# Sheaf and messages: 20 of each chunk's 125 columns are summed by source node in PSUM with one-hot matmuls, 105 are scatter-added

## The reference, cut to what matters

```python
# layer 1, "sheaf": a message for each end of each edge
msg_s = coef[:, None] * einsum('eij,ej->ei', L_sd, xd)
msg_d = coef[:, None] * einsum('eji,ej->ei', L_sd, xs)
out = x - zeros.at[src].add(msg_s) - zeros.at[dst].add(msg_d)
# layer 2, "messages": the index that is summed over is again src (row = edge_index[0])
m = silu(einsum('ei,ej,ijh->eh', x[dst], edge_attr, W_msg_tp) * norm)
agg = segment_sum(m, src)        # W_msg_lin is applied to the sums
```

## Time and profile before

| | |
|---|---|
| median of 3 runs | 31851.1 |
| lowest, highest | 31823.72, 31895.67 |
| the profiled execution's own time | 31882.81 |
| its span | 31881.0 |
| POOL busy | 24070.9 (76%) |
| DVE, PE, ACT busy | 9032.8 (28%), 8456.2 (27%), 1931.1 (6%) |
| PE's mean granted clock, 1.0 is 2.4 GHz | 0.651 |

### The profile page before, as it was taken

How to read it: one execution, slowest core, us unless ns; L and a number is a source line. 1 busy time by engine, 2 the same in 40 slices (tenths; PEclk the granted TensorE clock), 3 DMA queues, 4 the chain that set the end, 5 groups by cost and what they waited for, 6 DMA issues and landing times. The chain is left out here.

```text
span 31881.0 us, 172734 instructions
## 1 busy us (share of the span) xinstructions
PE 8456.2 (27%) x50463; PEld 7422.1 (23%) x50463; DVE 9032.8 (28%) x14173; ACT 1931.1 (6%) x4785; POOL 24070.9 (76%) x20072
## 2 busy tenths in 40 slices
PE   0000001000000644444444444244443443400003
PEld 0000001000000533333433333144443443200003
DVE  1434342111111433333333333121221211233332
ACT  0000000000000100000000000011111110000000
POOL 5777775777776788888888888778888886477776
PEclk9999998555555555555555555576676775655556
DMA  2111110111111111111111111222222221466664
GB/s 71 31 27 31 27 31 18 25 27 27 25 28 18 11 11 11 11 11 11 11 11 11 11 11 10 14 28 13 11 13 11 11 11 13 144 204 204 204 206 136
DMA packets 2304292, 1387.61 MB, mean 44 GB/s; under 512 B 1186461, under 2 KB 2150386, under 8 KB 2286402
## 3 DMA queue, kind: packets, MB, share of 16 engines
q0 software_dynamic: 1385008, 606.86, 16.8%
q10 hardware_dynamic: 814800, 576.02, 5.7%
q1 hardware_dynamic: 103746, 195.36, 1.8%
HBM read 666.59 MB, written 710.23 MB: 43 GB/s over the span
## 5 line engine op out<-in xcount | busy, mean ns | idle before, releaser
L1044 POOL DMA_INDIRECT acc<-column_sums,sum_rows x6250 | 10345.1, 1655 | 1936.1 <-issue 1879.4
L656 POOL DMA_INDIRECT gathered<-gat_table,src_index x6250 | 6525.8, 1044 | 2052.3 <-issue 2052.3
L1806 POOL DMA_INDIRECT gathered<-message_table,src_index x3125 | 3055.3, 978 | 984.7 <-issue 951.7
L1229 POOL DMA_INDIRECT gathered<-sheaf_table,src_index x3125 | 3011.5, 964 | 1026.4 <-issue 1025.3
L985 PE MATMUL column_sum<-edge_values,equal_src 128*128 128x16 f32 x6250 | 1363.6, 358 | 4857.3 <-ACT column_sums L1023 3410.7
L985 PEld LDWEIGHTS column_sum<-edge_values,equal_src 128*128 128x128 f32 x6250 | 1424.7, 332 | 4871.5 <-issue 3418.8
L511 PE MATMUL transposed<-ident,last_rows 128*128 128x128 f32 (+3 forms) x5 | 2.2, 442 | 8780.6 <-DVE sums L543 8780.6
L511 PEld LDWEIGHTS transposed<-ident,last_rows 128*128 128x128 f32 (+3 forms) x5 | 0.7, 149 | 8781.8 <-DVE sums L543 8781.8
L703 DVE TENSOR_TENSOR scores<-alpha_dst,gathered 128x375 f32<-128x375 f32 (+1 forms) x50 | 35.5, 710 | 6215.2 <-DMA gathered<-gat_table,src_index 6215.2
L998 DVE TENSOR_TENSOR equal_src<-src_row,src_chunk 128x512 f32<-128x512 f32 (+1 forms) x800 | 543.1, 679 | 4321.5 <-PE src_row L969 4304.3
L969 PE MATMUL src_row<-ident,src_chunk 128*128 128x128 f32 x6250 | 1559.5, 429 | 0.0
(11 more groups left out here) (335 smaller groups left out, 16084.8 us busy)
## 6 DMA issues: line engine op xcount, KB each, us to landing
message_rows<-gathered ACTq DMA_DIRECT2D x250, 1600.0 KB, 10.6
gathered<-gat_table,src_index POOLq DMA_INDIRECT x6250
acc<-column_sums,sum_rows POOLq DMA_INDIRECT x6250, 3.0
gat_rows<-scanned ACTq DMA_DIRECT2D x25, 3375.0 KB, 10.7
gat_rows<-scanned ACTq DMA_DIRECT2D x25, 2125.0 KB, 7.0
start_values<-starts SPq DMA_DIRECT2D x50, 1062.5 KB, 5.0
gathered<-sheaf_table,src_index POOLq DMA_INDIRECT x3125, 2.4
gathered<-message_table,src_index POOLq DMA_INDIRECT x3125, 2.9
```

The source lines that it names most:

```text
L656: g.indirect_dma_start(G[b][:, j, :], None, tab, bass.IndirectOffsetOnAxis(ap=IX[b][:, j:j + 1], axis=0)).then_inc(s_g[b], 16)
L1044: g.indirect_dma_start(self.acc[s * PER_SET + i], bass.IndirectOffsetOnAxis(ap=o.IXS[b][:, j:j + 1], axis=0), o.SV[b][:, j, :], None, comp ...
L1229: g.indirect_dma_start(G[b][:, j, :], None, self.tab17, bass.IndirectOffsetOnAxis(ap=IX[b][:, j:j + 1], axis=0)).then_inc(s_g[b], 16)
L1806: g.indirect_dma_start(G[b][:, j, :], None, self.qtab, bass.IndirectOffsetOnAxis(ap=IX[b][:, j:j + 1], axis=0)).then_inc(s_g[b], 16)
```

## The change

In both stages only the first 105 columns of a chunk (`SC`) go the old way. The last 20 (`MT`) are added in PSUM over the whole stage, in `o.acc`, four banks, 128 x 1568: partition is the low 7 bits of the source, the column is one of 16 features and one of 98 high parts. For each such column ("tile" below):

- DVE makes two one-hot matrices (`onehot`): low bits, 128x128 fp32, and high part, 128x98 bf16. Six small instructions per chunk split the sources into bits (`src_bits`).
- ACT writes the high one-hot times the edge's value for each of the 16 features (`place`: 16 activations of 98 columns, whose scale is a value per partition).
- PE multiplies (`tile_sum`: four fp32 matmuls of 392 columns, eight instructions).

The tiles of chunk k are worked in chunk k+1, the last chunk's after the stage. In the sheaf all 20 come in a row, between the hidden products and the equality groups, on both PE and ACT. In the messages one is put at the end of each of the first 20 steps on each engine. To make room in PSUM, the messages' four pairs of tiles (transposes, products, rows, sums) are single, and in the sheaf the rows share the two tiles of the hidden products, the sums share the tile of the transposes, and the second products have one tile. At the end of a stage DVE copies `o.acc` to SBUF, SP stores it as an eleventh accumulator, and `sum_accumulators` reads it too. The setup makes a row of 0 to 127.

```diff
+MT = 20
+SC = CH - MT
     def scatter_buffers(self, c, find_first):
-        o.groups = -(-CH // 4)
+        o.groups = -(-SC // 4)
+        o.NO = MT if find_first else 2
+        o.OL = sb("low_onehot", [P, o.NO, P])
+        o.OH = sb("high_onehot", [P, o.NO, NT], BF16)
+        o.MV = [sb(f"placed_values{b}", [P, D, NT]) for b in range(2)]
+        o.acc = self.ps("node_sums", [P, 4, 512], c)
+    def src_bits(self, v, w, o, src, b):
+        w(v.tensor_copy(o.LOI[:], src))
+        w(v.tensor_scalar(o.LOI[:], o.LOI[:], P - 1, None, ALU.bitwise_and))
+        w(v.tensor_copy(o.LO[b][:], o.LOI[:]))
...
+    def onehot(self, v, o, b, i):
+        r = i % o.NO
+        v.tensor_scalar(o.OL[:, r, :], self.iota_f[:], o.LO[b][:, i:i + 1], None, ALU.is_equal)
+        return v.tensor_scalar(o.OH[:, r, :], self.iota_f[:, 0:NT], o.HI[b][:, i:i + 1], None, ALU.is_equal)
+    def place(self, a, o, k, i, value):
+        n = k * MT + i
+        if not (first(k, 1) and i < 2):
+            a.wait_ge(o.s_tile, n - 1)
+        for d in range(D):
+            last = self.nc.scalar.activation(o.MV[i % 2][:, d, :], o.OH[:, i % o.NO, :], ACT.Copy, scale=value(d))
+        last.then_inc(o.s_mv, 1)
+    def tile_sum(self, pe, o, k, i):
+        n = k * MT + i
+        pe.wait_ge(o.s_mv, n + 1)
+        for m in range(4):
+            last = pe.matmul(o.acc[:, m, 0:4 * NT], o.OL[:, i % o.NO, :], o.MV[i % 2][:, 4 * m:4 * m + 4, :].rearrange("p d h -> p (d h)"),
+                             start=first(k, 1) and i == 0, stop=False, skip_group_check=True)
+        last.then_inc(o.s_tile, 1)
...
     def scatter_pool(self, g, o, k, b):
-        rounds = CH // PER_SET
+        rounds = SC // PER_SET
...
     def sheaf_edges   # PE, behind the eight groups of hidden products; ACT has tiles(k - 1) there too
+                        if not first(k, 1):
+                            tiles(k - 1)
                         self.scatter_pe(pe, o, k)
     # DVE, behind the copies of the gathered rows
+                        if not first(k, 1):
+                            onehots(k - 1, 1 - b, w)
+                        self.src_bits(v, w, o, srcc[:, SC:CH], b)
...
     def message_edges   # PE
-                        for s in range(GR + LAG):
+                        for s in range(GR + 1):
                             if s < GR:
                                 transposes(k, s)
+                            if s < GS:
                                 src_rows(k, s)
-                            if 1 <= s <= GR:
+                            if 1 <= s:
                                 second(k, s - 1)
-                            if s >= LAG:
+                            if LAG <= s < GS + LAG:
                                 sums(k, s - LAG)
+                            if s < MT and not first(k, 1):
+                                self.tile_sum(pe, o, k - 1, s)
     # ACT, last in its step s (before it: copy of transposes s, silu s-1, copy of sums s-3)
+                            if s < MT and not first(k, 1):
+                                placed(k - 1, s)
     # DVE, last in its step q (before it: outer product q, equality q)
+                            if q < MT and not first(k, 1):
+                                tile_onehot(k - 1, 1 - b, q)
```

More of the change, by code:

```diff
@@ L945, in scatter_buffers @@
         o.find_first = find_first
-        o.groups = -(-CH // 4)
-        o.VAL = sb("edge_values", [P, CH, D])
-        o.SV = [sb(f"column_sums{b}", [P, CH, D]) for b in range(2)]
-        o.IXS = [sb(f"sum_rows{b}", [P, CH], I32) for b in range(2)]
+        o.groups = -(-SC // 4)
+        if not find_first:
+            o.VAL = sb("edge_values", [P, CH, D])
+        o.SV = [sb(f"column_sums{b}", [P, SC, D]) for b in range(2)]
+        o.IXS = [sb(f"sum_rows{b}", [P, SC], I32) for b in range(2)]
         o.nq = 2 if find_first else 4
@@ new lines, in tile_sum, with keep_sums @@
+    def tile_sum(self, pe, o, k, i):
[5 more added lines that the diff above has]
+        last.then_inc(o.s_tile, 1)
+    def keep_sums(self, v, o):
+        v.wait_ge(o.s_tile, NCH * MT)
+        kept = o.MV[0][:].rearrange("p d h -> p (d h)").rearrange("p (h d) -> p h d", d=D)
+        for m in range(4):
+            v.tensor_copy(kept[:, :, 4 * m:4 * m + 4], o.acc[:, m, 0:4 * NT].rearrange("p (d h) -> p h d", d=4)).then_inc(o.s_out, 1)
@@ L1074, in _ @@
                     v.memset(zer[:], 0.0).then_inc(s_z, 1)
-                    for i in range(len(self.acc)):
+                    for i in range(len(parts)):
                         v.wait_ge(s_in[i % 2], 16 * (i // 2 + 1))
@@ L1248, in products @@
                             pe.wait_ge(s_xt, k * SG + (q + 1))
-                            if not first(k, 1) or q >= 2:
-                                pe.wait_ge(s_vc, k * SG + (q - 1))
+                            if not first(k, 1) or q >= 1:
+                                pe.wait_ge(s_vc, k * SG + q)
                             def second(j):
@@ L1265, in products, with tiles @@
                             second(3)
+                        if not first(k, 1):
+                            tiles(k - 1)
                         self.scatter_pe(pe, o, k)
+                    def tiles(k):
+                        pe.wait_ge(o.s_oh, k + 1)
+                        for i in range(MT):
+                            self.tile_sum(pe, o, k, i)
                     chunks(pe, NCH, 3, products)
+                    tiles(NCH - 1)
                 @block.scalar
@@ L1283, in step @@
                                 nc.scalar.activation(R[j % 2][:], pre[j % 2][:], ACT.Relu, bias=b1[:]).then_inc(s_r, 1)
+                        if not first(k, 1):
+                            tiles(k - 1, 1 - b)
                         self.scatter_act(a, o, k, b)
@@ L1286, in step, with tiles @@
                         a.dma_start(outv[:, ds(at, CH), :], OUT[b][:]).then_inc(s_o[b], 16)
+                    def tiles(k, b):
+                        a.wait_ge(o.s_oh, k + 1)
+                        for i in range(MT):
+                            self.place(a, o, k, i, lambda d: VP[b][:, i, d:d + 1])
                     chunks(a, NCH, 3, step)
+                    tiles(NCH - 1, (NCH - 1) % 2)
                     for b in range(2):
@@ L1298, in _, with onehots @@
                     K = [0]
+                    def onehots(k, b, w):
+                        if not first(k, 1):
+                            v.wait_ge(o.s_tile, k * MT)
+                        for i in range(MT):
+                            ins = self.onehot(v, o, b, i)
+                        w(ins)
+                        v.sem_inc(o.s_oh, 1)
                     def compute(k, b):
@@ L1454, in message_edges @@
             s_d0 = self.dsem("first_dst_in")
-            GR = o.groups
+            GR = -(-CH // 4)
+            GS = o.groups
             LAG = 3
@@ L1521, in second @@
                         pe.wait_ge(s_pt, k * GR + (q + 1))
-                        if not first(k, 1) or q >= 2:
-                            pe.wait_ge(s_ms, k * GR + (q - 1))
+                        if not first(k, 1) or q >= 1:
+                            pe.wait_ge(s_ms, k * GR + q)
                         for j in range(n):
-                            last = pe.matmul(mp[q % 2][:, j * D:(j + 1) * D], PT[q % 2][:, j * P:(j + 1) * P], Wm[:], start=True, stop=True)
+                            last = pe.matmul(mp[:, j * D:(j + 1) * D], PT[q % 2][:, j * P:(j + 1) * P], Wm[:], start=True, stop=True)
                         last.then_inc(s_m, 1)
                     chunks(pe, NCH, 3, products)
+                    for i in range(MT):
+                        self.tile_sum(pe, o, NCH - 1, i)
                 @block.scalar
@@ L1566, in _, with tile_onehot @@
                     K = [0]
+                    def tile_onehot(k, b, i):
+                        if not (first(k, 1) and i < 2):
+                            v.wait_ge(o.s_tile, k * MT + (i - 1))
+                        self.onehot(v, o, b, i).then_inc(o.s_oh, 1)
                     def compute(k, b):
@@ L1604, in _ @@
                     chunks(v, NCH, 3, compute)
+                    for i in range(MT):
+                        tile_onehot(NCH - 1, (NCH - 1) % 2, i)
+                    self.keep_sums(v, o)
     def layer3(self):
```

160 lines of the change are left out of this document (100 added, 60 removed).

## The result

The changed kernel takes 32560.0 us (median of 4 runs, 32523.07 to 32595.95), the kernel before 31838.97 beside it: 1.0224 of it, interval 1.0211 to 1.0236, or +721. The sign of the forecast was right and the time lies in its range, but only +324 had been forecast. The profiled execution took 32595.95, with a span of 32594.2.

A forecast was written before the change was run, and what follows sets the result against it. POOL bounds both stages; after the change, the messages' serial 12.4 step makes POOL wait. Sheaf -900, messages +1218, accumulator reads +6: +324 on 31882.8, 32207, median 32175; range 31265 to 33500.

The forecast's parts named there:

- the 40 in it: Sheaf: allowance for DVE's new small instructions holding up POOL, 40 taken between bounds of nothing and 300.
- The four terms: Messages step with a tile: PE's instructions 3.07, copy of sums 0.4, `place` 4.5, `tile_sum` 4.5, in series, 12.4.
- Terms 1 and 2: Messages step: PE's 28 instructions as before, 3.07 at 2.4 GHz; ACT's copy of the sums with hand-overs, 0.4.
- Term 3: Messages step: ACT's sixteen 98-column activations, 377 ns each at a pitch of 0.277, 4.5; bounds 3.1 and 6.0.
- B: Messages: `place` at the price without operand, 670 less, 31505; chance 10%.
- D: Messages: `place` activations without overlap, 720 more, 32895; chance 5%.
- within 16 ns: Claim that the Trainium skill's activation costs (186 ns, 0.833 per column, 93 per pointer operand) agree with the trace's rows.
- Term 4: Messages step: PE's eight 392-column instructions, 3.7 at the slow clock, then 2.4 x 0.33 = 0.8: 4.5; bounds 2.6 to 5.2.
- Chunk beside the tiles: Messages chunk outside its twenty tile steps: the other thirteen steps 34, the chunk's head on DVE 6.
- A: Messages: PE keeps its high clock, `tile_sum` 2.6 in place of 4.5, 912 less, 31265; chance 15%.
- C: Messages: PE stays at 1.2 GHz throughout, tile steps and other steps longer, 34625; chance 12%.
- E: Messages: the work overlaps after all and POOL stays the bound, step under 7.9, 30140; chance 3%.

## Why the prediction was right in sign and wrong in size

- **What bounds**: right. POOL ended last in both stages, and a chunk costs the longer of POOL's work and the others'. The ten-column runs and the later tile sum show both sides of that limit.
- **Sheaf**: forecast -900, measured -864, but the 40 in it were priced for the wrong thing. The small instructions cost POOL next to nothing; the gathers lost 209 because more of them lie beside the reflections, while fewer scatters do (1727 to 1704 ns each). The stage stayed POOL's; its slack fell from 212 to 113 a chunk, where 96 had been worked out. What the gathers and scatters took above their medians rose from 598 to 653, so that 40 was near the right size for a reason that wasn't in the prediction: luck.
- **Shape of the messages step**: right. The four terms follow one another; POOL waits for the copied sums and PE for `place`, as listed.
- **Terms 1 and 2**, 3.47 together: measured 12.96 - 4.38 - 5.26 = 3.32.
- **Term 3, `place`**: 4.5, measured 4.38. The operand's price and the overlap were read rightly from rows of another kind; rivals B and D are out. The prediction's "within 16 ns" holds for the 377 row alone: by the figures that it names there, the 285 row is 17 off and the 471 row 21.
- **Term 4, `tile_sum`: this step failed.** Forecast 4.5, measured 5.26. "3.7 slow, then 2.4 x 0.33" took one case of the hidden group, in which PE became fast after 3.5 of dense passes, for a fixed delay. Here the clock was low for 4.86 of a tile on the mean instead of 3.7, and nearly from end to end in 287 of 480. The upper bound of the term was off too: 3.54/4 x 392/512 is 0.68 and not 0.66, so eight slow passes make 5.4 by the rows, not 5.2, and such a tile measured 5.6. That the mean of 5.26 lies next to 5.2 is chance, since it mixes tiles of 5.6 with shorter ones. The matmuls with filler show the clock to be worth 2.34 a tile. The terms' errors are +0.76 here, -0.12 in `place` and -0.15 in terms 1 and 2: +0.49 against their unrounded sum of 12.47, +0.56 against the 12.4 that went into the chunk, and 480 x 0.56 = 269.
- **Chunk beside the tiles**: 40 forecast, (27456.7 - 20080.7 - 110)/24 = 302.7 for a chunk, less 20 x 12.96, is 43.5 measured: +84 in 24 chunks. The window of the chunk's head stands at a clock of 0.64; that this is its cause was not tested.
- **End of the stage**: the store took 12 and not 30; with what else differs at the two ends of the stage, which was not taken apart, -12 is left. The three make +341 (269 + 84 - 12), by which the stage missed its +1218.
- **Rivals**: A's clock was not there but could be had with filler; C was half true (PE cold in the tile, fast outside it); E was given 3% as part of this change, rightly, and became the best kernel once the order was altered.

With the term's stated upper end of 5.2 the forecast would have been 480 x 0.7 = 336 higher, 32511, close to the measured 32560 by the same chance.

## What to carry to other kernels

Work moved off the bounding engine is free only until the other engines' chain reaches it: work out that chain per chunk, and at the edge choose how much to move by it (here ten of 125 columns gained in any order, twenty only in the right one). When a producer and a consumer stand at the same place of two in-order queues, put the consumer one step later before anything else; it takes the pause away, and with it the slow clock behind the pause. Price a dense burst that follows a pause in every step at the low clock from end to end, and don't take the one place in a trace where the clock came back for a delay that holds elsewhere: here 287 of 480 bursts ran low nearly throughout. And look at which of POOL's instructions will lie beside DVE's long ones with two inputs; moving work shifts that too.

## What the runs showed of the hardware

- A tile of eight 392-column passes took 4.3 to 5.6 after PE had stood for 4.6 or more (5.6 in 287 of 480), 2.9 to 5.6 after pauses of mostly 1.8 (2.9 in 195 of 480), and 2.9 behind small matmuls without a pause (467 of 480); with filler in the pause, which left 1.0 of it, 2.9 in 474 of 480.
- More work made the kernel faster: 1839 of extra matmuls in PE's pauses took 1194 off the time.
- A gather took 0.95 with no DVE instruction of these kinds beside it and 2.43 on the mean beside a reflection instruction; a scatter 1.57 and 3.04. The Trainium skill (SBUF — State Buffer, "Who interferes with whom") says that tensor-scalar and copy instructions can block GpSimd for their whole length. Here they hardly did: beside the one-hots and the source bits a gather took 0.96 (10 of them) and a scatter 1.58 (144). Of the 653 by which the changed sheaf's gathers and scatters exceeded their medians (0.95, 1.55), 535 fell beside the reflections' instructions with two inputs and 74 beside scans.
- An activation of 1568 columns with a pointer scale took 1.60, sixteen of 98 columns 4.38: 1.02 ns a column against 2.8, fixed parts included.
